# A three-layer graph attention kernel: where a chunk's maxima are started, how its sums are drained, and from where ACT's copies of G come

## The chip, the cores and the metric

One core of a Trainium2 chip. The metric is device time in microseconds of one execution, the median of the runs.

## The reference

Three graph attention layers over N = 3125 nodes, 128 features wide (the hidden width of the first is 256), with 103125 edges and one loop more per node. Cut to what matters:

```python
def gat_layer(x, src, dst, W, a_src, a_dst, b):
    h = x @ W
    e = leaky_relu((h @ a_src)[src] + (h @ a_dst)[dst], 0.2)
    ex = exp(e - segment_max(e, dst)[dst])
    alpha = ex / segment_sum(ex, dst)[dst]
    return segment_sum(alpha[:, None] * h[src], dst) + b

h = relu(layernorm(x))
x = x + gat_layer(relu(gat_layer(h, ..., W1)), ..., W2)     # layers 0 and 1
h = relu(layernorm(x))
x = x + gat_layer(h, ..., W3)                               # layer 2
```

## The kernel before, in words

**Counts.** The first part turns the edge list into a dense matrix C of counts (how often node i points at node j), kept in SBUF as bytes, 125 partitions by 25 tiles by 5 chunks of 625 destinations. The change leaves it alone; it ends at some 242 us.

**Layers.** Each of the 3 layers (L) walks over NC = 5 chunks (c) of 625 destinations, and each chunk over T = 25 steps (s), one per tile of 125 sources. A step needs a tile of weights, 125 sources by 625 destinations: max(r_src, G) times the count, where G is a row of one number per destination, the same on all partitions. DVE makes 15 of the 25 tiles in one instruction each (`product`, L903), from G in PSUM, which TensorE has spread over the partitions by five transposes (`fast_rows`, L1335). For the 10 steps in POOL_S, ACT makes the maximum in three instructions (`row_maximum`, L1135, L1138, L1140) from a copy of G in SBUF (`ga`), and POOL multiplies by the count (`blocks`, L479). The copy: TensorE transposes once more (`copied_rows`, L1344, after step COPY_PE = 6), ACT moves the rows to SBUF (`copy_rows`, L1147, after step COPY_ACT = 8). TensorE then multiplies the tile with the sources' features (`products`, L1354): five destination tiles, two records each in the trace, so ten a step, summed in PSUM over the 25 steps. The tiles lie in a ring of 8 buffers (and a ninth for step 24); DVE and ACT wait on `pe_done` before they overwrite one.

**Maxima.** Each chunk also needs a maximum over all sources: 25 `top_step` instructions of DVE (L777, L780) run into two PSUM buffers, TOP0 and TOP1. A step waits for the last one of its own buffer (`same`), `in_odd` says which buffer it has. `join_tops` (L785) joins the two. `fast_chunk` of DVE starts them AHEAD = 4 steps ahead of the products, two of them after the chunk's last product. TensorE transposes the result (`top_transpose`, L1313, after step 1 of the next chunk, for the last chunk after step 23), DVE reduces it and works out `back` in four parts at the steps CHAIN_AT (`maxima`, L793 to L807); ACT makes `kappa` of it (`factors`, L1056, step 9).

**Drain.** ACT copies the sums from PSUM to `raw` (`move_sums`, L1051 and L1052) at step 3 of the next chunk, behind the row maximum of step 2, once all 25 steps are done; TensorE's step 0 waits for it (`drained`). DVE then makes `rz` in three parts at steps 9, 10 and 11 (`sums_inverse`, L818 to L831). In layer 1 DVE adds the sums to x at step 12 (`residual`, L838, five instructions) and takes the statistics of the layer norm at 13 and 14; POOL works out the scale (L458 to L463), ACT normalises (L1089). Layers 0 and 1 also compute the next layer's features between TensorE's steps (`after_sums`: L1371, L1379, L1387, L1400, L1403).

**Order.** Every engine runs its instructions in the order in which the program lists them: in ACT's `fast_chunk` the row maximum of a step stood ahead of what follows the sums. `fast_rows` for the next chunk comes after TensorE's step ROWS_PE = 23, and waits for all of DVE's products of the chunk, since these read the same PSUM rows. SP only stores the result in layer 2.

## Time and profile before

| what | us |
|---|---|
| median of 3 runs (lowest, highest) | 861.53 (860.94, 868.83) |
| the profiled execution's own time | 867.72 |
| its span in the trace | 866.0 |
| mean granted TensorE clock, share of full speed | 0.904 |
| DVE busy / PE busy / ACT busy / POOL busy | 748.6 / 705.4 / 495.7 / 269.8 |

Numbers of rows are microseconds from the start of the span unless marked ns. Busy times are the sums of an engine's instructions; PE and PEld (its weight loads) overlap.

### The profile page before, as it was taken

The page shows a single profiled execution, that of the slowest core. Times are in us where ns is not written, and L with a number is a line of the kernel's source. Part 1 is how long each engine was busy: PE and PEld are TensorE (multiplying, and loading weights), DVE is VectorE, ACT ScalarE, POOL GpSimd, SP SyncE. Part 2 cuts the span into 40 slices and gives each one's busy share as a digit, 9 for nine tenths or more (in the row PEclk, how much of TensorE's full clock was granted, in tenths as well). Part 3 has the DMA queues.
Part 4 walks back from the last instruction along what each step waited for, and adds up shares of the span by engine and source line. Part 5 has one row for each costly group of instructions (what it writes and reads, how often), then busy time and mean ns, then how long its engine had stood idle before and what let it go on. Part 6 is the DMA issues. An engine that isn't in the chain of part 4 may idle for free.

```text
span 866.0 us, 14422 instructions
## 1 busy us (share of the span) xinstructions
PE 705.4 (81%) x5762; PEld 681.2 (79%) x5762; DVE 748.6 (86%) x1010; ACT 495.7 (57%) x790; POOL 269.8 (31%) x214
## 2 busy tenths in 40 slices
PE   5256889988878898989957989797984798988984
PEld 5256888888868898989957979797974798978984
DVE  5599999999789989898729899989892989999993
ACT  0072444444478765686527856757662787585671
POOL 1512000000025434343303434434340245462563
PEclk9996788888789999999958999898987799999997
DMA  3400000000000000000000000000000000000001
GB/s 97 95 1 1 1 1 1 2 1 1 1 1 2 1 2 1 1 2 1 2 3 1 1 1 2 2 1 1 2 0 4 1 2 1 16 17 1 16 1 33
DMA packets 9554, 6.86 MB, mean 8 GB/s; under 512 B 2108, under 2 KB 9145, under 8 KB 9470
## 3 DMA queue, kind: packets, MB, share of 16 engines
q1 hardware_dynamic: 8670, 4.49, 1.9%
q0 software_dynamic: 800, 1.26, 0.6%
q8 instruction: 52, 0.85, 0.4%
q14 instruction: 32, 0.26, 0.1%
HBM read 4.14 MB, written 1.60 MB: 7 GB/s over the span
## 4 chain that ended last, share of the span: by engine, by line
PE 47%; DVE 30%; issue 9%; ACT 6%; POOL 5%; DMA 2%; DVEq 0%; POOLq 0%; ACTq 0%
PE ps L1354 30%; DVE scratch L617 13%; DVE ps L777 7%; PE ps L1256 7%; DVE scratch L903 4%; POOL scratch L479 2%; ACT scratch L1140 2%; PE ps L1400 2%; PE ps L1216 2%; ACT scratch L1135 1%; PE ps L1379 1%; DMA edge_sb<-in_edges 1%; PE ps L1335 1%; PE ps L1344 1%; PE ps L1263 1%
## 5 line engine op out<-in xcount | busy, mean ns | idle before, releaser
L1354 PE MATMUL ps<-hA,scratch 125*125 125x129 f32 x2500 | 303.4, 280 | 36.3 <-POOL scratch L479 20.9
L1354 PEld LDWEIGHTS ps<-hA,scratch 125*125 125x125 f32 x2500 | 291.2, 192 | 45.5 <-POOL scratch L479 25.2
L479 POOL TENSOR_TENSOR scratch<-scratch 125x625 f32<-125x625 f32 x150 | 209.8, 1402 | 302.5 <-ACT scratch L1140 302.5
L777 DVE SCALAR_TENSOR_TENSOR ps<-C,a_unit,ps 125x625 f32<-125x625 uint8 x330 | 276.1, 860 | 0.5
L903 DVE SCALAR_TENSOR_TENSOR scratch<-ps,r_src,C 125x625 f32<-125x625 f32 x225 | 191.6, 858 | 23.3 <-PE ps L1335 23.3
L1354 PE MATMUL ps<-hB,scratch 125*125 125x129 f32 x1250 | 162.2, 291 | 27.5 <-DVE scratch L903 15.7
L1354 PEld LDWEIGHTS ps<-hB,scratch 125*125 125x125 f32 x1250 | 155.1, 203 | 32.9 <-DVE scratch L903 18.8
L1256 PE MATMUL ps<-scratch 128*128 128x125 bf16 x1250 | 148.4, 296 | 23.3 <-DVE scratch L617 17.2
L1256 PEld LDWEIGHTS ps<-scratch 128*128 128x128 bf16 x1250 | 143.0, 121 | 27.6 <-DVE scratch L617 21.2
L1140 ACT ACTIVATE scratch<-scratch,r_src 125x625 f32<-125x625 f32 x150 | 134.8, 899 | 0.0
L1003 ACT ACTIVATE C<-ps 125x1750 uint8<-125x1750 f32 (+3 forms) x50 | 74.3, 1488 | 98.4 <-PE ps L1256 98.4
L1135 ACT ACTIVATE scratch<-gathered,r_inv 125x625 f32<-125x625 f32 x150 | 121.2, 808 | 0.8 <-PE ps L1354 0.8
L1138 ACT ACTIVATE scratch<-C 125x625 f32<-125x625 uint8 x150 | 107.4, 716 | 4.8 <-POOL scratch L479 4.8
L617 DVE TENSOR_TENSOR scratch<-key_lo,hB 128x6656 bf16<-128x6656 bf16 (+3 forms) x26 | 94.6, 3640 | 4.2 <-PE ps L1256 4.1
L617 DVE TENSOR_TENSOR scratch<-key_col,hB 128x6500 bf16<-128x6500 bf16 (+3 forms) x26 | 85.9, 3304 | 0.0
L470 POOL PARTITION_ALL_REDUCE extg<-ext x3 | 2.8, 926 | 189.1 <-DVE ext L637 189.1
L1147 ACT ACTIVATE gathered<-ps 125x625 f32<-125x625 f32 x15 | 10.4, 692 | 56.0 <-PE ps L1344 56.0
L1051 ACT ACTIVATE scratch<-ps 125x387 f32<-125x387 f32 x15 | 7.4, 492 | 48.4 <-PE ps L1354 48.4
L780 DVE TENSOR_SCALAR ps<-C,a_unit 125x625 f32<-125x625 uint8 x30 | 24.8, 862 | 4.3 <-issue 4.2
L793 DVE TENSOR_REDUCE mu<-ps 125x5 f32<-125x625 f32 x15 | 12.0, 803 | 15.7 <-PE ps L1313 15.7
L634 DVE TENSOR_SCALAR a_neg<-ab 125x25 f32<-125x25 f32 x3 | 0.5, 180 | 28.3 <-ACTq L1205 23.8
L1089 ACT ACTIVATE scratch<-xr,nbias,rstd 125x128 f32<-125x128 f32 x25 | 10.2, 483 | 25.7 <-POOL nbias L463 25.7
(146 smaller groups left out, 478.2 us busy)
## 6 DMA issues: line engine op xcount, KB each, us to landing
xr<-in_x SPq DMA_DIRECT2D x1, 1562.5 KB
out<-xr SPq DMA_DIRECT2D x5, 312.5 KB
edge_sb<-in_edges SPq DMA_DIRECT2D x1, 805.7 KB
w<-in_W SPq DMA_DIRECT2D x2, 128.0 KB
gathered<-in_edges,start_i POOLq DMA_INDIRECT x5, 6.3
w<-in_W SPq DMA_DIRECT2D x1, 64.0 KB
av<-in_a_src SPq DMA_DIRECT2D x4, 0.5 KB
av<-in_a_dst SPq DMA_DIRECT2D x4, 0.5 KB
```

Of the source, the lines that this page charges most:

```text
L479: g.tensor_tensor(slot[s], slot[s], wide[n % 2], ALU.mult).then_inc(pool_done[L], 1)
L617: last = v.tensor_tensor(hot[:, g0:g1, :, :], keys.unsqueeze(2).broadcast_to([128, g1 - g0, m, LANES]), iota_t[:, 0:m, :].unsqueeze(1).bro ...
L777: v.scalar_tensor_tensor(dest, counts, a_unit[:, s:s + 1], top, ALU.min, ALU.max).then_inc(top_done[L], 1)
L780: v.tensor_scalar(dest, counts, a_unit[:, s:s + 1], None, ALU.min).then_inc(top_done[L], 1)
L903: v.scalar_tensor_tensor(slot[s].rearrange("p (t n) -> p t n", n=P), tiles(ROWU), r_src[:, s:s + 1], C5[:, c, s, :].rearrange("p (t n) -> ...
L1003: a_.activation(C5[:, c, :, rows].rearrange("p t (w q) -> p t w q", q=WQ), tiles(at_, w1_ - w0).rearrange("p w (t q) -> p t w q", q=WQ), A ...
L1135: a_.activation(A, ga[c % 2][:, :], ACT.Relu, bias=-1.0, scale=r_inv[:, s:s + 1]).then_inc(over_done[L], 1)
L1138: a_.activation(wide[k % 2], C5[:, c, s, :], ACT.Copy)
L1140: a_.activation(A, A, ACT.Identity, bias=r_src[:, s:s + 1], scale=r_src[:, s:s + 1]).then_inc(rowmax_ok[L], 1)
L1216: last = mm(ps[0:P, CNT + g:CNT + g + 1], before[:, k, P * g:P * (g + 1)], ones_b[:, :], start=(k == 0 and g == 0), stop=(k == NS - 1), sk ...
L1256: last = mm(ps[0:128, o:o + WC], hot_lo[i][:, at_g, :, lane], hot_col[i][:, at_g, :, lane], start=(k == 0), stop=(k == KC - 1))
L1354: last = mm(ps[0:P, acc_at(t):acc_at(t) + HW], A[:, P * t:P * (t + 1)], feat, start=opens and t in (0, 3), stop=closes, skip_group_check=True)
```

## The change

- `in_odd` loses its cases: steps 0 to 4 of a chunk's maxima all go to TOP0, from step 5 on odd ones to TOP1. AHEAD is 5: these five run back to back after a chunk's last product (before the first product, in a layer's first chunk); the other twenty are spread over the steps 0 to 22 by `top_at`, the join follows at step 23.
- The products of steps 23 and 24 are issued together, first both steps for destination tiles 0 to 2, then both for 3 and 4 (`last_products`); a semaphore `acc_half` tells ACT when the first three are done. ACT moves the sums at step 0 instead of 3. `fast_rows` comes after step 22, and the last chunk's `top_transpose` after step 24.
- In ACT's `fast_chunk` the move, `factors` and `after_sums` stand ahead of the row maximum of their step. POOL_S is (3, 5, 7, 9, 11, 14, ...) instead of (2, 4, 6, 9, 11, 13, ...).
- In layer 1, chunks 0 to 3, POOL makes the residual (a product and a sum, 125x640 each) behind its tile of step 11; the statistics move to the steps 15 and 16.
- Only chunk 0's copy of G is made by TensorE and ACT. TensorE transposes g_row to 25 lines of 125, ACT copies them out, SP stores them in DRAM and loads each later chunk's 625 numbers back onto all 125 partitions, as soon as the buffer is free. SP reads the mode flag for it, and DVE waits for that reading before it writes the next.

```diff
+    g_d = nc.dram_tensor("g_lines", (3, T * P), fp32).ap()
-        AHEAD = 4
-        SUMS_AT = 3
+        AHEAD = 5
+        SUMS_AT = 0
-        TOPS_PE, LAST_TOPS = 1, 23
+        TOPS_PE, LAST_TOPS = 1, 24
-        COPY_PE, COPY_ACT = 6, 8
-        ROWS_PE = 23
+        ROWS_PE = 22
-        RESIDUAL_AT, STATS = 12, (13, 14)
-        POST_POOL = [((12, 0),), ((15, 3),), ((12, 0), (15, 1), (18, 2))]
+        STATS = (15, 16)
+        POST_POOL = [((12, 0),), ((12, 2), (17, 3)), ((12, 0), (15, 1), (18, 2))]
-        POOL_S = (2, 4, 6, 9, 11, 13, 16, 18, 20, 22)
+        POOL_S = (3, 5, 7, 9, 11, 14, 16, 18, 20, 22)
-        def in_odd(c, k):
-            if c == 0 and k < AHEAD:
-                return False
-            return k % 2 == (AHEAD - 2) % 2 if k < AHEAD else k > AHEAD and k % 2 == (AHEAD + 1) % 2
+        def in_odd(k):
+            return k >= AHEAD and k % 2 == 1
+        def top_at(k):
+            return (k - AHEAD) * (T - 3) // (T - 1 - AHEAD)
...
+            def ga_load(L, c):
+                if c > 1:
+                    sp.wait_ge(over_done[L], pool_no(c - 1, 0))
+                    sp.wait_ge(ga_loaded[L], 16 * (c - 1))
+                sp.dma_start(ga[c % 2], g_d[L, c * CD:(c + 1) * CD].unsqueeze(0).broadcast_to([P, CD])
+                             ).then_inc(ga_loaded[L], 16)
+            for L in range(LAYERS):
+                sp.wait_ge(mode_ready, L + 1)
+                mode = sp.value_load(fast[0:1, 0:1], min_val=0, max_val=1)
+                sp.sem_inc(mode_read, 1)
+                with sp.If(mode):
+                    sp.wait_ge(lines_ready[L], 1)
+                    sp.dma_start(g_d[L, :].rearrange("(t p) -> t p", p=P), g_lines).then_inc(lines_stored[L], 16)
+                    sp.wait_ge(lines_stored[L], 16)
+                    ga_load(L, 1)
+                    for c in range(NC):
+                        if 0 < c < NC - 1:
+                            ga_load(L, c + 1)
+                        if L == LAYERS - 1 and c:
+                            store(c - 1)
...
+            def residual(c):
+                pool.wait_ge(rz_ready, NC + c + 1)
+                g.tensor_tensor(agg, raw[:, :, 0:D], rz[:, :].unsqueeze(2).broadcast_to([P, CT, D]),
+                                ALU.mult).then_inc(raw_used, 1)
+                pool.wait_ge(raw_used, NC + c + 2)
+                xc = xr[:, c * CT:(c + 1) * CT, :]
+                g.tensor_tensor(xc, xc, agg, ALU.add).then_inc(x_ready, 1)
...
             def fast_chunk(L, c):
                 for s in range(T):
                     if s not in POOL_S:
                         product(L, c, s)
-                    if s or c == 0:
-                        next_top(L, c * T + s + AHEAD)
-                    if s == T - 1:
-                        next_top(L, (c + 1) * T + AHEAD)
+                    for k in range(AHEAD, T):
+                        if top_at(k) == s:
+                            top_step(L, c, k)
+                    if s == top_at(T - 1) + 1:
+                        join_tops(L, c)
...
+                if c < NC - 1:
+                    for k in range(AHEAD):
+                        top_step(L, c + 1, k)
...
-            def move_sums(L, c):
+            def move_sums(L, c, halves=True):
                 n = L * NC + c
-                act.wait_ge(pe_done[L], in_layer(c, T))
                 act.wait_ge(raw_used, n + 1)
+                if halves:
+                    act.wait_ge(acc_half[L], c + 1)
+                else:
+                    act.wait_ge(pe_done[L], in_layer(c, T))
                 a_.activation(raw[:, 0:3, :], acc3[0], ACT.Copy).then_inc(raw_half, 1)
+                if halves:
+                    act.wait_ge(pe_done[L], in_layer(c, T))
                 a_.activation(raw[:, 3:CT, :], acc3[1], ACT.Copy).then_inc(raw_ready, 1)
...
+            def copy_rows(L):
+                act.wait_ge(ga_rows[L], 1)
+                a_.activation(g_lines, ps[0:T, work_at(CT):work_at(CT) + P], ACT.Copy).then_inc(lines_ready[L], 1)
+                a_.activation(ga[0].rearrange("p (t n) -> p t n", n=P), tiles(WORK), ACT.Copy).then_inc(ga_ready[L], 1)
...
-                    if s in POOL_S:
-                        row_maximum(L, c, s)
                     if c:
                         if s == SUMS_AT:
                             move_sums(L, c - 1)
                         if s == KAPPA_AT:
                             factors(L, c - 1)
                         after_sums(L, c - 1, s)
-                    if NP and s == COPY_ACT and c < NC - 1:
-                        copy_rows(L, c + 1)
+                    if s in POOL_S:
+                        row_maximum(L, c, s)
...
+            def last_products(L, c):
+                for t0, t1, out_sem in ((0, 3, acc_half[L]), (3, CT, pe_done[L])):
+                    for s in (T - 2, T - 1):
+                        for t in range(t0, t1):
+                            last = mm(ps[0:P, acc_at(t):acc_at(t) + HW], slot[s][:, P * t:P * (t + 1)],
+                                      h_of[L][:, s, :], start=False, stop=s == T - 1, skip_group_check=True)
...
-                    if NP and s == COPY_PE and c < NC - 1:
-                        copied_rows(L, c + 1)
```

## Rows read from the trace of the kernel before

**Rows 1.** The page: busy time, share of the span and instructions of each engine

```profile
PE 705.4 (81%) x5762; PEld 681.2 (79%) x5762; DVE 748.6 (86%) x1010; ACT 495.7 (57%) x790; POOL 269.8 (31%) x214
```

**Rows 2.** The waits: us in total, times, longest us

```profile
ACT gathered L1147 <- PE ps L1344: 56.0, 15, 4.7
...
PE ps L1354 <- POOL scratch L479: 32.5, 22, 2.6
...
DVE scratch L903 <- PE ps L1335: 23.3, 9, 3.8
...
DVE zk L818 <- ACT kappa L1056: 9.1, 12, 1.0
```

**Rows 3.** SP's waits, in the same columns

```profile
SPq L60 <- DMA out<-xr: 4.7, 1, 4.7
```

**Rows 4.** Timeline: the drains that bound three chunks of layers 0, 1 and 2

```profile
281.35 0.49 ACT L1051 ACTIVATE scratch<-ps 125x387 f32<-125x387 f32 x1 [3.45 <-PE ps L1354]
...
397.26 0.49 ACT L1051 ACTIVATE scratch<-ps 125x387 f32<-125x387 f32 x1 [0.85 <-PE ps L1354]
...
493.55 0.49 ACT L1051 ACTIVATE scratch<-ps 125x387 f32<-125x387 f32 x1 [3.45 <-PE ps L1354]
...
614.99 0.49 ACT L1051 ACTIVATE scratch<-ps 125x387 f32<-125x387 f32 x1 [0.85 <-PE ps L1354]
...
713.64 0.49 ACT L1051 ACTIVATE scratch<-ps 125x387 f32<-125x387 f32 x1 [3.45 <-PE ps L1354]
...
820.38 0.49 ACT L1051 ACTIVATE scratch<-ps 125x387 f32<-125x387 f32 x1 [6.16 <-PE ps L1354]
```

**Rows 5.** Stretches: us, PE, PEld, DVE, ACT, POOL busy (records), PEclk, DMA share, GB/s

```profile
280.30:318.50 38.20, 35.15 (x313) 34.40 (x312) 34.63 (x48) 25.95 (x43) 13.69 (x10) 1.00 0.00 1
...
572.90:614.00 41.10, 35.13 (x283) 34.09 (x282) 37.47 (x64) 26.42 (x45) 15.80 (x14) 0.92 0.01 1
```

**Rows 6.** Timeline around the boundary of layer 1's chunk 3: DVE and PE

```profile
572.94 1.64 DVE L903 SCALAR_TENSOR_TENSOR scratch<-ps,r_src,C 125x625 f32<-125x625 f32 x2 [2.64 <-PE ps L1335]
...
574.61 2.44 PE L1354 MATMUL ps<-hB,scratch 125*125 125x129 f32 x20 [0.68 <-DVE scratch L903]
```

**Rows 7.** Timeline of the same chunk: the copy of G and what follows it

```profile
583.67 0.69 ACT L1147 ACTIVATE gathered<-ps 125x625 f32<-125x625 f32 x1 [4.71 <-PE ps L1344]
...
586.56 1.50 POOL L479 TENSOR_TENSOR scratch<-scratch 125x625 f32<-125x625 f32 x1 [6.00 <-ACT scratch L1140]
586.68 1.40 DVE L818 TENSOR_TENSOR zk<-scratch,kappa 125x5 f32<-125x5 f32 x1 [0.95 <-ACT kappa L1056]
...
588.12 5.77 PE L1354 MATMUL ps<-hB,scratch 125*125 125x129 f32 x50 [2.28 <-POOL scratch L479]
```

**Rows 8.** A stretch of the same chunk, columns as in rows 5

```profile
600.00:604.00 4.00, 3.80 (x18) 3.50 (x18) 4.00 (x6) 4.00 (x9) 2.23 (x3) 0.50 0.00 0
```

**Rows 9.** Timeline of DVE in the last chunks of layers 0 and 1

```profile
396.22 1.64 DVE L903 SCALAR_TENSOR_TENSOR scratch<-ps,r_src,C 125x625 f32<-125x625 f32 x2 [2.54 <-PE ps L1335]
...
424.16 2.41 DVE L903 SCALAR_TENSOR_TENSOR scratch<-ps,r_src,C 125x625 f32<-125x625 f32 x3
...
613.96 1.64 DVE L903 SCALAR_TENSOR_TENSOR scratch<-ps,r_src,C 125x625 f32<-125x625 f32 x2 [2.57 <-PE ps L1335]
...
632.97 1.39 DVE L838 SCALAR_TENSOR_TENSOR xr<-scratch,rz,xr 125x128 f32<-125x128 f32 x5
...
645.73 2.41 DVE L903 SCALAR_TENSOR_TENSOR scratch<-ps,r_src,C 125x625 f32<-125x625 f32 x3
```

**Rows 10.** Timeline: three maxima of one buffer in a row

```profile
242.82 2.69 DVE L777 SCALAR_TENSOR_TENSOR ps<-C,a_unit,ps 125x625 f32<-125x625 uint8 x3
```

**Rows 11.** The groups by line: POOL's sum in layer 2

```profile
L498 POOL TENSOR_TENSOR xr<-xr,scratch 125x640 f32<-125x640 f32 x5 | 6.6, 1319 | 0.1
```

**Rows 12.** Timeline of the end of layer 0

```profile
432.85 1.27 PE L1354 MATMUL ps<-hA,scratch 125*125 125x129 f32 x10
433.05 0.81 DVE L793 TENSOR_REDUCE mu<-ps 125x5 f32<-125x625 f32 x1 [6.47 <-PE ps L1313]
...
435.12 0.17 DVE L818 TENSOR_TENSOR zk<-scratch,kappa 125x5 f32<-125x5 f32 x1 [0.54 <-ACT kappa L1056]
```

More of the change, by code:

```diff
@@ L273, in gat_stack_kernel @@
         kappa_ready = sem("kappa_ready")
+        x_ready = sem("x_ready")
         raw_half = sem("raw_half")
+        acc_half = [sem(f"acc_half{L}") for L in range(3)]
         raw_ready = sem("raw_ready")
@@ L310, in gat_stack_kernel @@
         ga_ready = [sem(f"ga_ready{L}") for L in range(3)]
+        ga_loaded = [sem(f"ga_loaded{L}") for L in range(3)]
+        lines_ready = [sem(f"lines_ready{L}") for L in range(3)]
+        lines_stored = [sem(f"lines_stored{L}") for L in range(3)]
+        mode_read = sem("mode_read")
         h1_sb = sem("h1_sb")
@@ L351, in in_layer @@
             return c * T + s
[L354 removed]
+        POOL_S = (3, 5, 7, 9, 11, 14, 16, 18, 20, 22)
         NP = len(POOL_S)
[L357 to L362 removed]
+        def in_odd(k):
+            return k >= AHEAD and k % 2 == 1
+        LAST_ODD = max(k for k in range(T) if in_odd(k))
+        def top_at(k):
+            return (k - AHEAD) * (T - 3) // (T - 1 - AHEAD)
         def pool_before(s):
@@ L416, in store @@
                 sp.dma_start(out_v[:, bass.ds(c * CT, CT), :], xr[:, bass.ds(c * CT, CT), :]).then_inc(out_done, 16)
-            for L in range(LAYERS - 1):
-                with sp.Fori(0, NC) as c:
-                    rest_loads(L, c)
-            for c in range(NC):
-                rest_loads(LAYERS - 1, c)
-                if c:
-                    store(c - 1)
+            def ga_load(L, c):
[18 more added lines that the diff above has]
+                            store(c - 1)
+                with sp.Else():
+                    for c in range(NC):
+                        rest_loads(L, c)
+                        if L == LAYERS - 1 and c:
+                            store(c - 1)
             store(NC - 1)
@@ L508, in post @@
                     result(c, part)
+                elif part == 2:
+                    residual(c)
                 else:
@@ L544, in _ @@
                     for _at, part in POST_POOL[L]:
-                        post(L, NC - 1, part)
+                        if (L, part) != (1, 2):
+                            post(L, NC - 1, part)
         @block.vector
@@ L762, in top_step @@
                 n = c * (T + 1)
-                odd = in_odd(c, s)
+                odd = in_odd(s)
                 at_ = TOP1 if odd else TOP0
                 top = ps[0:P, at_:at_ + CD]
-                same = [k for k in range(s) if in_odd(c, k) == odd]
+                same = [k for k in range(s) if in_odd(k) == odd]
                 if same:
@@ L857, in after_sums @@
                 if L == 1:
-                    if s == RESIDUAL_AT:
-                        residual(c)
                     if s == STATS[0]:
@@ L1130, in row_maximum @@
                 n, A = in_layer(c, s), slot[s]
-                act.wait_ge(ga_ready[L], c + 1)
                 k = pool_no(c, s)
+                if c:
+                    act.wait_ge(ga_loaded[L], 16 * c)
+                else:
+                    act.wait_ge(ga_ready[L], 1)
                 if c or s >= RING:
-                    act.wait_ge(pe_done[L], n - RING if s < RING else n - (RING - 1) if s < T - 1 else n - (T - 1))
-                a_.activation(A, ga[c % 2][:, :], ACT.Relu, bias=-1.0, scale=r_inv[:, s:s + 1]).then_inc(over_done[L], 1)
+                    act.wait_ge(pe_done[L], n - RING if s < RING else n - (RING - 1))
+                a_.activation(A, ga[c % 2], ACT.Relu, bias=-1.0, scale=r_inv[:, s:s + 1]).then_inc(over_done[L], 1)
                 if k > 1:
@@ L1182, in _ @@
                     if NP:
[L1183 removed]
+                        copy_rows(L)
                     for c in range(NC):
@@ L1356, in products @@
                 last.then_inc(out_sem, 1)
+            def last_products(L, c):
[4 more added lines that the diff above has]
+                                      h_of[L][:, s, :], start=False, stop=s == T - 1, skip_group_check=True)
+                        if t1 == CT:
+                            last.then_inc(out_sem, 1)
+                    if t1 < CT:
+                        last.then_inc(out_sem, 1)
             def rest_steps(L, c):
@@ L1363, in rest_steps, with feat_transposes @@
                                  rest_pe, False, False)
-            def feat_transposes(L, c, source, ready, n, maxima_of, rows_of=0):
+            def feat_transposes(L, c, source, ready, n, maxima_of):
                 pe.wait_ge(ready, n)
                 pe.wait_ge(top_max[L], maxima_of + 1)
-                if NP and rows_of:
-                    pe.wait_ge(ga_ready[L], rows_of)
                 for t in range(CT):
@@ L1445, in fast_chunk @@
                         pe.wait_ge(h_scaled[L], s + 1)
-                    products(slot[s], h_of[L][:, s, :], pe_done[L], s == 0, s == T - 1,
-                             L * NC + c if c and s == 0 else 0)
+                    if s < T - 2:
+                        products(slot[s], h_of[L][:, s, :], pe_done[L], s == 0, False,
+                                 L * NC + c if c and s == 0 else 0)
+                    elif s == T - 1:
+                        last_products(L, c)
                     if c:
```

54 lines of the change are left out of this document (23 added, 31 removed).

## The prediction, made before the changed kernel ran

> **What bounds the kernel now.** I read the page first: DVE is busy 86% of the span, PE 81%, the others far less [rows 1]. With two engines that close, the shares don't say what a stage is worth, so I went on to the waits. The reader should find four there that the change touches [rows 2]: DVE waits 23.3 us in 9 places for the spread rows of G; ACT waits 56.0 us for the transposes of its own copy of G; PE waits 32.5 us for POOL's tiles; DVE waits 9.1 us for kappa. Then the drains as milestones: three chunks take 397.26 - 281.35 = 115.9 us in layer 0, 614.99 - 493.55 = 121.4 in layer 1 and 820.38 - 713.64 = 106.7 in layer 2 [rows 4], so 38.6, 40.5 and 35.6 a chunk. Last the timeline of one chunk of layer 1. At its boundary DVE, which has no other work in its program, sits 2.64 us until the rows come, and PE then sits 0.68 for the drain and the first product [rows 6]. Half way, ACT waits 4.71 us in order to copy G; its next row maximum is late, POOL idles 6.00 us, PE 2.28 us and DVE 0.95 us [rows 7]. Later the same chunk has a stretch at a granted clock of 0.50, that is at 1.2 GHz, with 18 records in 4 us, where 50 took 5.77 us before it [rows 7, 8]. So in layers 0 and 1 neither engine is the bound alone: each has 34 to 37 us of work in 38 to 41, and they wait for each other in turn. Layer 2 is close to what DVE alone needs.
>
> **The change part by part.**
>
> *DVE's floor.* The last chunks show DVE without a boundary in them. Layer 0: from 396.22 to 424.16 + 2.41 = 426.57, 30.35 us; layer 1: from 613.96 to 648.14, 34.18 us [rows 9]. Each holds 21 maxima; the new chunk has 20 before its last product and 5 behind it. One DVE instruction of this size takes 0.78 us behind another (two take 1.64, one about 0.86) [rows 6]; but the five all go to one buffer and each waits for the one before, as three did in 2.69, so 0.90 each, 4.5 us [rows 10]. Layer 0: 30.35 - 0.78 + 4.5 = 34.1. Layer 1 loses the residual too, 1.39: 34.18 - 1.39 - 0.78 + 4.5 = 36.5. Layer 2 has no residual and no statistics; I take layer 0's figure and add for the one instruction more in its inverse and for blocked ones (below): 34.9. Were the five as quick as others, each chunk would be 0.6 shorter.
>
> *The rows at the boundary.* After its last product DVE now has 4.5 us of maxima, not two (1.6 us). PE's five transposes are issued one step of ten records (1.1 us) earlier. The wait of 2.64 was what was left after 1.6 us of cover; 4.5 - 1.6 + 1.1 = 4.0 more covers it, and the longest, 3.8, too. What is late next is PE itself where it has no slack.
>
> *PE's floor in layer 0.* A chunk has 313 records in 35.15 us [rows 5], 0.112 each. The copy's five go: 34.6. The early drain takes the 0.68: DVE's first product is ready when PE has done its 20 last records (2.2 us), and ACT's move of the first half (0.49, [rows 4]) fits under the second half's 8 records. The 2.28 us behind the copy goes, but the row maximum of step 9 now stands behind kappa, which waits for DVE's `back` of step 7: kappa 0.2, row maximum 2.1, POOL 1.5, 3.8 us behind `back`, where PE wants the tile after some 2.7; I put 1.1 us for it (bounds 0 and the old 2.28). Sum 34.6 + 1.1 = 35.7, and 0.1 for hand-overs: 35.8 a chunk, above DVE's 34.1. So layer 0 gains 115.9 - 3 x 35.8 = 8.5 us.
>
> *Layer 1.* PE has 283 records [rows 5], about 31.5 us at full clock, and then waits for POOL: the residual puts 2 x 1.32 us [rows 11] ahead of the tile of step 14, and the norm's scale ahead of step 18, each later for PE by up to 1.5 us. PE has 5 us of slack for that, so DVE's 36.5 stands, if the clock holds. With a stretch at 1.2 GHz in it I reckon 38. Bounds 36.5 and 38.5; I take 37.2, nearer to the first: 121.4 - 111.6 = 9.8 us.
>
> *Layer 2.* 106.7 - 3 x 34.9 = 2.0 us.
>
> *The first chunks.* Three boundaries lose a wait of 2.6 on average (23.3 / 9) [rows 2]. ACT loses the copy and the wait for it. Ahead of the first product stand a fifth maximum (0.9, on the path) and a small transpose and copy of G's lines (between 0.2 and 0.7; ACT has time for it). 2.0 each, 6.0 us. Bounds 3 and 9.
>
> *The last chunks.* PE ended layer 0 at 434.12, and zk came at 435.12 [rows 12], 1.0 later, since the maxima had been transposed one step earlier. Now the five transposes follow the last product (0.7), then the chain from L793 to zk, 2.07 us: 2.8 less 0.2 for the earlier move. PE's end is 0.6 earlier, as the transposes left its way: 1.0 us lost a layer, 3.0 in all. In return the last chunk of layer 1 loses a residual on DVE and a good part of its slow stretch, 3.4 us, that of layer 2 gains 1.3, that of layer 0 nothing. Net +1.7 us (bounds -3 and +5).
>
> *The transfer.* SP has nothing else to do until layer 2's stores. The only transfer of this size whose landing shows is the last store: SP waits 4.7 us for it [rows 3]. The load is asked for when the chunk's predecessor's row maxima are done, a whole chunk (35 us) before it is needed; even five times the store's 4.7 us, 24 us, would hide. Cost 0 (bounds 0 and 1 for SP's reading of the flag, which DVE waits for only one layer later). Without the cover, each would cost its landing. POOL's other idle time hides the residual.
>
> **A rule against moving the residual.** DVE's zk, five numbers a partition, took 1.40 us while POOL's tile ran from 586.56 to 588.06, and 0.17 when POOL was idle [rows 7, 12]. So an instruction of DVE can lose a whole POOL instruction. The Trainium skill, SBUF — State Buffer, section "Who interferes with whom", has it as a rule: a DVE instruction with two SBUF inputs and a GpSimd instruction that reads SBUF exclude each other for the whole instruction. This trace agrees. By that rule the residual saves DVE nothing if its time comes back as such waits, which is the second rival below.
>
> **The sum.** 8.5 + 9.8 + 2.0 + 6.0 + 1.7 = 28.0 us. The profiled execution took 867.72 us (span 866.0 and 1.7 around it), so it would take 839.7. The median of the runs is 861.53, 6.2 below; the same gain gives 833.5 us, 3.3% less. A measurement of this kernel can tell about 1% from no change.
>
> **The rivals.**
>
> *PE becomes the bound at a falling clock (0.25).* In layers where DVE leads, PE now waits at the boundary for the last product, does 25 records, and waits again for the first product behind five maxima: 4.5 + 0.86 - 0.7 - 2.2, about 2.4 us idle, each chunk. Such a wait (2.28), followed by another, came before the stretch at 0.50 [rows 7, 8]. Against it: a PE that lags has no such gap. If it costs 1.7 us in each chunk of layer 0, 1.8 in layer 1 and 1 in layer 2 over my figures, 3 x 4.5 = 13.5 us come back: 847. [...]
>
> *DVE is blocked by a denser POOL (0.12).* So far POOL is idle when DVE's small instructions of steps 5 to 7 run; without the copy's stall it isn't. One blocked instruction more in each of the 12 later chunks at 1.2 us: 14 us back, 848. Against it: the last chunks, which have no copy, held one or two such waits and are in my floors.
>
> *The wait only moves (0.07).* The rows now come before PE's last two steps, so the next step 0 is later by 1.1 us, and if that and step 9's wait are not hidden under DVE, layers 0 and 1 keep their pace: only the first chunks' 6 and layer 2's 2, less the tail's 3, about 5 us: 856.
>
> *Slower (0.06).* The same gap at the boundary, but with PE at 1.2 GHz for so long that the ring of 8 is full and DVE stops. Each record costs 0.11 us more; 45 slow records are 5 us. In layer 1 PE has 31.5 us of work at full clock and some 3 us of waits; from 55 slow records on (of 283), 34.5 + 6 passes the old 40.5. With 75 a chunk in all layers I get 34.5 + 8.3 = 42.8 in layer 1, 43 in layer 0 and 38 in layer 2: 3 x (4.4 + 2.3 + 2.4) = 27 worse, less 5: 883. I see no such run of slow records now, hence the low chance.
>
> **How the numbers follow.** My forecast has 0.50, its own range 827 to 841. Faster by over 1%: the forecast, the first two rivals (0.87), less a little for their far ends: 0.86. Within 1%: 0.08. Slower: 0.06. The lower end of the range takes layer 1 at 36.5 (2), step 9 without a gap in layer 0 (3), the first chunks' and tail's better bounds (4): about 824. The upper end takes in the falling clock and the blocked DVE: 851.
>
> **What would show it.** Right: DVE's wait for the rows all but gone (under 4 us in place of 23.3); no wait of ACT for transposes of a copy but one a layer; drains 35 to 36 us apart in layer 0, about 37 in layer 1, 35 in layer 2; five maxima at 0.9 in a row; the mean clock at or over 0.90; the gap from PE's last product to zk 2.6 us. Wrong: PE's waits for POOL at step 9 still above 2 us; zk, rz or m_top at 1.4 us oftener than once a chunk; ACT's first row maximum of a chunk waiting for SP's load; more stretches at 0.50 right behind the boundaries.

## The result, and the profile after

| | before | after |
|---|---|---|
| median (lowest to highest), us | 861.24 (858.94 to 868.83), 4 runs | 833.63 (833.27 to 834.56), 4 runs |
| profiled execution; its span, us | 867.72; 866.0 | 833.74; 831.8 |
| mean granted clock | 0.904 | 0.923 |

The ratio is 0.9658, 95% interval 0.9615 to 0.9702: faster, and the median lies 0.1 us from the forecast. The profiled executions gained 34.0 us, though, where my sum had 28.0. Both can't be right for the reasons that I gave, and most of what follows is about that.

The page of the changed kernel: busy times, and the clock in 40 slices.

```profile
PE 680.1 (82%) x5705; PEld 658.9 (79%) x5705; DVE 739.7 (89%) x990; ACT 490.1 (59%) x781; POOL 270.2 (32%) x222
...
PEclk9996887889779999999998999999996799999997
...
gathered<-g_lines SPq DMA_DIRECT2D x12, 305.2 KB
```

PE has 57 records less, DVE 20 instructions less (the residual, five in each of four chunks) [rows 1]. Its waits (us in total, times, longest):

```profile
PE ps L1396 <- POOL scratch L506: 28.3, 22, 1.5
...
DVE scratch L945 <- PE ps L1379: 5.1, 6, 1.4
...
ACT gathered L1193 <- PE ps L1386: 3.8, 2, 2.1
...
DVE zk L858 <- ACT kappa L1101: 1.0, 3, 0.3
```

Against [rows 2], DVE's wait for the rows fell from 23.3 to 5.1, ACT's for the copy from 56.0 to 3.8 and DVE's for kappa from 9.1 to 1.0. Under 4 us was what I had named for the rows; it is 5.1. PE's wait for POOL hardly moved: 32.5 to 28.3. No compute engine waits for SP's twelve loads; SP itself waits for them to land, 26.7 us in all and 4.1 us at the longest.

One middle chunk of layer 0 and one of layer 1 (columns as in [rows 5]):

```profile
313.70:349.90 36.20, 34.69 (x308) 34.06 (x308) 34.59 (x48) 25.75 (x43) 14.57 (x11) 1.00 0.03 10
551.80:588.10 36.30, 31.89 (x277) 30.75 (x277) 35.86 (x58) 25.91 (x43) 17.68 (x16) 1.00 0.00 1
```

In layer 0 PE is busy 34.69 of 36.2 us, with 308 records; in layer 1 DVE is busy 35.86 of 36.3. The clock is full in both, where layer 1 before had 0.92. The timeline of the first of them, PE, DVE, ACT and POOL, tells what is left:

```profile
309.58 3.60 DVE L817 SCALAR_TENSOR_TENSOR ps<-C,a_unit,ps 125x625 f32<-125x625 uint8 x4
...
314.28 2.37 PE L1405 MATMUL ps<-hA,scratch 125*125 125x129 f32 x20
314.55 0.87 DVE L945 SCALAR_TENSOR_TENSOR scratch<-ps,r_src,C 125x625 f32<-125x625 f32 x1 [1.37 <-PE ps L1379]
315.86 0.49 ACT L1094 ACTIVATE scratch<-ps 125x387 f32<-125x387 f32 x1 [2.13 <-PE ps L1405]
...
325.16 0.21 ACT L1101 ACTIVATE kappa<-back 125x5 f32<-125x5 f32 x1 [1.74 <-DVE back L847]
...
327.37 0.16 DVE L858 TENSOR_TENSOR zk<-scratch,kappa 125x5 f32<-125x5 f32 x1
...
327.57 1.51 POOL L506 TENSOR_TENSOR scratch<-scratch 125x625 f32<-125x625 f32 x1 [2.78 <-ACT scratch L1188]
...
329.13 4.67 PE L1396 MATMUL ps<-hA,scratch 125*125 125x129 f32 x40 [1.49 <-POOL scratch L506]
329.69 1.29 POOL L506 TENSOR_TENSOR scratch<-scratch 125x625 f32<-125x625 f32 x1 [0.61 <-ACT scratch L1188]
329.84 1.16 DVE L871 TENSOR_TENSOR rz<-zk,kappa 125x5 f32<-125x5 f32 x1
```

Three things are to be seen. The dependent maxima run at 0.90 us (four in 3.60), yet DVE still waits 1.37 us for the rows. PE's only gap, 1.49 us, comes from ACT, which waits for `back` ahead of kappa and has step 9's row maximum behind it. And zk, which took 1.40 us before in nine of fifteen chunks, takes 0.16; but rz, five numbers a partition as well, now takes 1.16 beside the POOL tile that began at 329.69.

To find where the time went I use DVE's zk as a mark, and PE's first rows of a layer:

```profile
291.23 0.16 DVE L858 TENSOR_TENSOR zk<-scratch,kappa 125x5 f32<-125x5 f32 x1
...
399.65 0.16 DVE L858 TENSOR_TENSOR zk<-scratch,kappa 125x5 f32<-125x5 f32 x1
...
426.98 0.17 DVE L858 TENSOR_TENSOR zk<-scratch,kappa 125x5 f32<-125x5 f32 x1 [0.34 <-ACT kappa L1101]
...
442.59 0.80 PE L1379 MATMUL ps<-ident,g_row 125*125 125x125 f32 x5 [3.98 <-ACT e_src L1063]
...
491.75 0.16 DVE L858 TENSOR_TENSOR zk<-scratch,kappa 125x5 f32<-125x5 f32 x1
...
600.95 0.16 DVE L858 TENSOR_TENSOR zk<-scratch,kappa 125x5 f32<-125x5 f32 x1
...
628.50 0.17 DVE L858 TENSOR_TENSOR zk<-scratch,kappa 125x5 f32<-125x5 f32 x1 [0.34 <-ACT kappa L1101]
```

| gain in us, layers 0 / 1 / 2 | predicted | first profile of before | third profile of before (below) |
|---|---|---|---|
| first rows to first zk | 2.0 / 2.0 / 2.0 | 2.7 / 3.7 / 3.8 | 2.9 / 3.8 / 3.8 |
| three middle chunks | 8.5 / 9.8 / 2.0 | 7.4 / 12.2 / 3.5 | 7.5 / 8.6 / 3.6 |
| last chunk to its zk | -1.0 / 2.4 / 0.3 | -2.1 / 1.6 / -1.0 | -2.1 / -0.3 / -1.0 |
| between the layers, both gaps | 0 | 2.7 | 1.8 |
| sum | 28.0 | 34.5 | 28.5 |

### The profile page after: what moved, and what is told of

Read it like the earlier page. It is cut to its first block, busy times and chain, and to the rows that moved or that the text cites. A ratio compares the mean times of both kernels' runs of the same rounds, so it can differ in the third digit from the quotient of the medians.

```text
span 831.8 us, 14225 instructions
## 1 busy us (share of the span) xinstructions
PE 680.1 (82%) x5705; PEld 658.9 (79%) x5705; DVE 739.7 (89%) x990; ACT 490.1 (59%) x781; POOL 270.2 (32%) x222
## 4 chain that ended last, share of the span: by engine, by line
DVE 43%; PE 32%; issue 12%; ACT 7%; POOL 4%; DMA 2%; DVEq 0%; POOLq 0%; ACTq 0%
DVE ps L817 16%; PE ps L1396 14%; DVE scratch L655 13%; PE ps L1300 7%; DVE scratch L945 7%; PE ps L1405 2%; ACT scratch L1188 2%; DVE ps L820 2%; PE ps L1260 2%; POOL scratch L506 2%; PE ps L1452 1%; PE ps L1431 1%; ACT scratch L1183 1%; DMA edge_sb<-in_edges 1%; ACT scratch L1134 1%
## 5 line engine op out<-in xcount | busy, mean ns | idle before, releaser
L1396 PE MATMUL ps<-hA,scratch 125*125 125x129 f32 x2300 | 273.9, 279 | 29.2 <-DVE scratch L945 17.1
L506 POOL TENSOR_TENSOR scratch<-scratch 125x625 f32<-125x625 f32 x150 | 200.1, 1337 | 292.4 <-ACT scratch L1188 283.6
L1396 PEld LDWEIGHTS ps<-hA,scratch 125*125 125x125 f32 x2300 | 265.1, 192 | 35.7 <-DVE scratch L945 20.2
L817 DVE SCALAR_TENSOR_TENSOR ps<-C,a_unit,ps 125x625 f32<-125x625 uint8 x330 | 279.1, 863 | 1.9
L945 DVE SCALAR_TENSOR_TENSOR scratch<-ps,r_src,C 125x625 f32<-125x625 f32 x225 | 193.6, 860 | 5.1 <-PE ps L1379 5.1
L1300 PE MATMUL ps<-scratch 128*128 128x125 bf16 x1250 | 148.4, 296 | 23.3 <-DVE scratch L655 17.1
L1300 PEld LDWEIGHTS ps<-scratch 128*128 128x128 bf16 x1250 | 143.0, 121 | 27.6 <-DVE scratch L655 21.1
L1396 PE MATMUL ps<-hB,scratch 125*125 125x129 f32 x1150 | 139.4, 279 | 22.4 <-POOL scratch L506 16.3
L1396 PEld LDWEIGHTS ps<-hB,scratch 125*125 125x125 f32 x1150 | 132.8, 191 | 27.8 <-POOL scratch L506 20.6
L1101 ACT ACTIVATE kappa<-back 125x5 f32<-125x5 f32 x15 | 3.1, 207 | 42.7 <-DVE back L847 42.7
L1405 PE MATMUL ps<-hA,scratch 125*125 125x129 f32 x200 | 23.7, 273 | 0.2 <-DVE scratch L945 0.2
```

What stands on the lines that cost most here:

```text
L506: g.tensor_tensor(A, A, wide[n % 2], ALU.mult).then_inc(pool_done[L], 1)
L817: v.scalar_tensor_tensor(dest, counts, a_unit[:, s:s + 1], top, ALU.min, ALU.max).then_inc(top_done[L], 1)
L945: v.scalar_tensor_tensor(slot[s].rearrange("p (t n) -> p t n", n=P), tiles(ROWU), r_src[:, s:s + 1], C5[:, c, s, :].rearrange("p (t n) -> ...
L1300: last = mm(ps[0:128, o:o + WC], hot_lo[i][:, at_g, :, lane], hot_col[i][:, at_g, :, lane], start=(k == 0), stop=(k == KC - 1))
L1396: last = mm(ps[0:P, acc_at(t):acc_at(t) + HW], A[:, P * t:P * (t + 1)], feat, start=opens and t in (0, 3), stop=closes, skip_group_check=True)
L1405: last = mm(ps[0:P, acc_at(t):acc_at(t) + HW], slot[s][:, P * t:P * (t + 1)], h_of[L][:, s, :], start=False, stop=s == T - 1, skip_group_c ...
```

## The experiments

Twelve runs: nine edited kernels, the changed kernel once more and the kernel before twice more. The kernel before was timed beside each group. "The changed kernel" is the one predicted (833.6 us; 834.4 in its second series). A chunk's period is read from one zk to the next.

**1. The transfer undone.** PE and ACT copy G for every chunk, as before, after steps 6 and 8; the rest stays changed. Cut to what matters:

```diff
-                            ga_load(L, c + 1)
...
+                    if s == 8 and c < NC - 1:
+                        copy_rows(L, c + 1)
...
+                    if s == 6 and c < NC - 1:
+                        copied_rows(L, c + 1)
```

> The changed kernel with ACT's copies of G made as before (five transposes after step 6, ACT's copy at step 8, no transfer). My theory: PE does 5 records more a chunk (0.6 us), and ACT's copy stands ahead of kappa and the row maximum of step 9, so PE's wait for POOL there grows from 1.49 to about 3 us. Layers 0 and 1, where PE's end sets the boundary, lose about 2 us a chunk, layer 2 nothing, the first chunks 1.5 each: 849 us, 15 over the 833.6 (bounds 843 to 854). Rival, the boundary is all and the copy's stall was hidden anyway: at most 837.

848.15 us (844.69 to 849.31); ratio to before 0.9772 (0.9714 to 0.9830). Its waits:

```profile
ACT gathered L1186 <- PE ps L1382: 41.2, 15, 4.8
PE ps L1392 <- POOL scratch L500: 39.3, 21, 2.6
...
DVE scratch L939 <- PE ps L1374: 18.4, 9, 4.9
```

The size is as I expected, the places are not. Layer 0 lost 3.0 us in its first middle chunk and 1.4 in the others (37.6 against 36.14), the first chunks 2.3 to 2.7 each, and 3.2 us were lost between layers 0 and 1 (taken up below). But layer 1's middle chunks took 36.2 (two of them 36.13) and layer 2's 34.22, slightly less than with the transfer (36.40 and 34.67): beside the later POOL tile rz took 0.69 us in layer 1, not 1.16, and 0.51 in layer 2, not 0.96. In the middle chunks where DVE leads, the copy cost nothing.

**2. The residual back on DVE**, five instructions at step 12; POOL's part, (12, 2), goes.

```diff
-        POST_POOL = [((12, 0),), ((12, 2), (17, 3)), ((12, 0), (15, 1), (18, 2))]
+        POST_POOL = [((12, 0),), ((17, 3),), ((12, 0), (15, 1), (18, 2))]
...
+                    if s == 12:
+                        residual(c)
```

> The changed kernel with layer 1's residual back on DVE at step 12 (the statistics stay at 15 and 16). My theory: layer 1 is bound by DVE, 1.39 us more in each of 4 chunks, a little less where PE was the last: 838 us, 4.5 over the 833.6 (bounds 836.5 to 840). Rival, the rule of the shared port: what DVE saved comes back as blocked instructions and a late POOL, so no difference, 833 to 834.5.

844.35 us (843.41 to 847.86), ratio 0.9755 (0.9698 to 0.9812): more than my upper bound. DVE and POOL at that step:

```profile
534.46 1.29 POOL L506 TENSOR_TENSOR scratch<-scratch 125x625 f32<-125x625 f32 x1 [0.83 <-ACT scratch L1186]
535.12 2.89 DVE L878 SCALAR_TENSOR_TENSOR xr<-scratch,rz,xr 125x128 f32<-125x128 f32 x5
536.58 1.29 POOL L506 TENSOR_TENSOR scratch<-scratch 125x625 f32<-125x625 f32 x1 [0.83 <-ACT scratch L1186]
```

The five took 1.39 us in the last chunk of the kernel before [rows 9] and 1.58 to 1.59 in its middle chunks, and 2.89 here for each of the chunks 0 to 3, where they lie across two tiles; for chunk 4's own sums, behind the layer's last product with POOL idle, they took 1.40. A chunk of layer 1 took 39.18 us, 2.8 more. So the blocking that I held against the move speaks for it: in this denser kernel the residual on DVE costs twice its own time. The Trainium skill, SBUF — State Buffer, section "Who interferes with whom", has it that a DVE instruction with two inputs in SBUF and a GpSimd (POOL) instruction that reads SBUF contend for ports that they share, and that these are an exclusive lock. These rows agree: the first of the five took 0.78 us and the fifth 1.41, against 0.34 for each of the three between.

**3. The early drain undone**: the last two steps in the old order, one wait ahead of ACT's two copies.

```diff
-            def move_sums(L, c, halves=True):
+            def move_sums(L, c, halves=False):
...
-                for t0, t1, out_sem in ((0, 3, acc_half[L]), (3, CT, pe_done[L])):
-                    for s in (T - 2, T - 1):
...
+                for s in (T - 2, T - 1):
+                    products(slot[s], h_of[L][:, s, :], pe_done[L], False, s == T - 1)
```

> The changed kernel without the early drain: steps 23 and 24 one after the other, the move of the sums waits for both. My theory: ACT's move (0.49 us and its hand-overs) shows again as about 0.7 us of PE's time a chunk, on the path in layer 0 and mostly in layer 1, hidden in layer 2: 838 us (bounds 836 to 840). Rival, the drain lies beside DVE's product: 833.6, within 1.

838.69 us (837.03 to 840.30), ratio 0.9671 (0.9615 to 0.9726). The total fits, but only 0.4 us a chunk were lost in layer 0 (36.53) and 0.5 in layer 1 (36.88), nothing in layer 2 (34.67); 2.9 us of its 6.2 us longer span lie between layers 0 and 1. I had put 0.68 on it. Not all of the rest is PE's wait for the drain, either: with the chunk's start shifted, DVE's e_top and m_top lay beside tiles of POOL and took 0.37 us longer between them, 0.65 in one chunk of layer 1, and that chunk lost 0.66 where the other two lost 0.38 and 0.39. In layer 1, where DVE leads, this accounts for the whole loss; in layer 0 the two parts are not told apart.

**4. The rows two steps later.**

```diff
-        ROWS_PE = 22
+        ROWS_PE = 24
```

> The changed kernel with the spread rows of G issued behind the products of steps 23 and 24 (ROWS_PE 24) instead of behind step 22; the five maxima at the boundary stay. My theory: the rows come 2.2 us later; layer 1 has 0.3 of DVE's wait now and gets 2.1 to 2.5, layer 0 has PE wait 0.9 for the first product, layer 2 covers all: 4 x 2 + 4 x 0.9 = 11 us, 845 us (bounds 840 to 848). Rival, the five maxima are the whole cover and the place of the rows is nothing: at most 836.

849.21 us (847.70 to 850.92), ratio 0.9797 (0.9741 to 0.9852), above my upper bound. DVE at a boundary of layer 1:

```profile
526.32 0.87 DVE L945 SCALAR_TENSOR_TENSOR scratch<-ps,r_src,C 125x625 f32<-125x625 f32 x1 [2.62 <-PE ps L1379]
```

Two steps are 20 records, 2.2 us, and each boundary of layers 0 and 1 lost just that: chunks of 38.35 and 38.57 us, waits of 3.57 and 2.5 us. There was no spare cover in either layer. In layer 2 (34.67) there was.

**5. Three maxima at the boundary, not five.**

```diff
-        AHEAD = 5
+        AHEAD = 3
```

> Three maxima of the next chunk behind the last product, not five; the two others go back among the products, where they are not dependent on one another. The rows still come one step early. My account: the cover was the sum of both, 4.0 us over what the old wait needed, and the changed kernel's own trace shows 1.37 us of wait left in layer 0 and 0.3 in layer 1. Two maxima less are 1.8 us less cover, but DVE's last product is then about 1.6 us later against the same rows, so the wait hardly changes: 833.6 plus or minus 1.5 us, the wait for the rows at 1.4 to 2.0 us in layer 0. Rival, the five maxima are themselves what hides the rows: each of 12 boundaries loses up to 1.8 us, 845 to 855 us, and DVE's waits for the rows come back to over 15 us in all.

841.48 us (839.90 to 843.77), ratio 0.9731 (0.9668 to 0.9793). My account failed. The time lies between it and the rival's, and the rival had DVE's waits for the rows right: 15.6 us in all. DVE behind its last product in layer 1:

```profile
515.68 1.78 DVE L817 SCALAR_TENSOR_TENSOR ps<-C,a_unit,ps 125x625 f32<-125x625 uint8 x2
519.70 0.87 DVE L945 SCALAR_TENSOR_TENSOR scratch<-ps,r_src,C 125x625 f32<-125x625 f32 x1 [2.23 <-PE ps L1379]
```

With five maxima DVE worked 5 x 0.90 and waited 0.30 us, 4.8 in all; with three it worked 3 x 0.90 and waits 2.1 to 2.2, 4.8 to 4.9 again. In layer 1 the rows come 4.8 us behind DVE's last product either way, so each maximum that is taken from there opens the wait by its own time, and comes back among the products: 37.8 us a chunk, 1.4 more. In layer 0 the rows' place moved (5.8 us behind the last product with five, 5.0, 6.6 and 5.0 with three), the waits were 2.4, 4.0 and 2.4 us, and the chunks took 36.8, 38.4 and 36.8. In layer 2 the chunk even gained 0.3 (34.4), and the first chunks 1.0 each. Another 3.2 us of loss lie between layers 0 and 1 (18.8 us against 15.6).

**6. Row maximum ahead of kappa at step 9.**

```diff
-                        if s == KAPPA_AT:
-                            factors(L, c - 1)
                         after_sums(L, c - 1, s)
                     if s in POOL_S:
                         row_maximum(L, c, s)
+                    if c and s == KAPPA_AT:
+                        factors(L, c - 1)
```

> ACT takes step 9's row maximum first and kappa behind it, in place of the other way round. In the changed kernel PE waits 1.49 us at step 9 of every later chunk for POOL's tile. My account (PE is the bound in layer 0, and that gap is 1.1 of its 35.8 us): the gap goes, and layer 0 gains about 1.2 us in each of 4 chunks, layer 1 and 2 under 0.3 a chunk, since DVE leads there: 828 us (826 to 830). zk may be blocked by POOL's tile again or wait for kappa, which costs DVE up to 1.2 us a chunk. Rival (the gap is slack that PE gives back elsewhere, DVE is the bound in layer 0 too): within 1 us of 833.6.

824.55 us (824.42 to 825.15), ratio 0.9533 (0.9475 to 0.9592): 9.1 us better than the changed kernel, and below the range that I had given. Its stretches (a chunk of layer 0, one of layer 1), then its rz:

```profile
312.91:347.45 34.54, 34.52 (x307) 34.00 (x306) 33.59 (x49) 25.60 (x43) 14.58 (x11) 1.00 0.03 10
544.43:579.78 35.35, 32.09 (x277) 30.86 (x276) 34.86 (x59) 25.79 (x43) 17.70 (x16) 1.00 0.00 1
```

```profile
329.01 0.16 DVE L871 TENSOR_TENSOR rz<-zk,kappa 125x5 f32<-125x5 f32 x1
```

In layer 0 PE is now busy 34.52 of 34.54 us: the gap was on the path, all of it. Layer 1 gained 1.0 us a chunk, which I had not expected: POOL's tile ends before rz, so rz takes 0.16 us in place of 1.17, and DVE leads there. In layer 2 rz fell from 0.96 to 0.16 too, but a chunk gained only 0.2, for another of DVE's small instructions met a tile of POOL in its place:

```profile
L836 DVE SCALAR_TENSOR_TENSOR e_top<-mu,span,b_low 125x5 f32<-125x5 f32 x1 | 0.8, 833 | 0.0
```

It had taken 225 ns there in the changed kernel (the group of that line, one chunk of layer 2).

**7. The last maxima transposed behind step 23 again.**

```diff
-        TOPS_PE, LAST_TOPS = 1, 24
+        TOPS_PE, LAST_TOPS = 1, 23
```

> Only the last chunk of each layer: PE transposes the joined maxima behind step 23 again, ahead of the last products, not behind them. My account put 1.0 us a layer on this: zk 1.0 us earlier behind PE's last product in each layer, 830.6 us (829.5 to 832). Rival (the transposes only delay PE's last products and these set the end): no gain, 833.6.

828.74 us (828.20 to 830.55), ratio 0.9587 (0.9527 to 0.9646). zk came 1.1, 1.1 and 1.8 us earlier in the last chunks; 1.8 us more came from between layers 0 and 1. PE's end and zk in layer 0:

```profile
423.16 2.37 PE L1405 MATMUL ps<-hA,scratch 125*125 125x129 f32 x20
...
426.14 0.17 DVE L858 TENSOR_TENSOR zk<-scratch,kappa 125x5 f32<-125x5 f32 x1 [1.26 <-ACT kappa L1101]
```

Here zk comes 0.6 us behind PE's last product; in the changed kernel it was 426.98 - 424.53 = 2.45.

**8. The five maxima alternating between the two buffers.**

```diff
-        def in_odd(k):
-            return k >= AHEAD and k % 2 == 1
...
+        def in_odd(c, k):
+            if k < AHEAD:
+                return bool(c) and k in (0, 2)
+            return k % 2 == 1
```

> The five maxima behind the last product alternate between the two PSUM buffers again, so that none waits for the one right before it. They take 0.90 us each in the changed kernel and should take 0.79: 0.5 us less at each boundary. My account: DVE leads in layers 1 and 2, so 8 boundaries gain 0.4 to 0.5 us; in layer 0 the rows are late anyway and the wait grows by what the maxima lose: 830 us (829 to 832). Rival (the rows bound all three layers): within 1 us of 833.6, and the wait for the rows grows by 0.5 at every boundary.

837.03 us (834.13 to 838.67), ratio 0.9671 (0.9607 to 0.9734). The rival's mechanism held in layers 0 and 1: the chunks kept their pace (36.16 and 36.42), and the wait for the rows grew by 0.4 us at each boundary, to 1.77 in layer 0 and 0.72 to 0.82 in layer 1. Its time did not: the median is 3.4 us above the changed kernel's, not within 1. Of the profiled span's 3.2 us more, 2.0 lie between layers 0 and 1; in layer 2, which has no such wait, a chunk took 34.79, 0.1 more, and e_top 0.73 us in place of 0.22.

**9. Edits 6 and 7 together, and the changed kernel again beside it.**

> Both edits that gained alone: ACT's row maximum of step 9 ahead of kappa (9.1 us by the medians) and the last chunk's maxima transposed behind step 23 (4.9 us, of which 1.8 was the clock behind layer 0). They touch different chunks, so they should add: 36.16 - 1.6 a chunk in layer 0, 36.36 - 1.0 in layer 1, and zk 1.1 us (layers 0 and 1) and 1.8 us (layer 2) earlier in the last chunks. 824.6 - 4.0 = 820.6 us, between 818.5 and 822.5 by what the clock does behind layer 0. Rival (the last chunk's gain comes from the same wait of PE): 823 to 825.

> The changed kernel unaltered, beside the kernel before on the same chip as the best version. If the 833.6 us belong to the kernel and not to one chip: 832 to 836 us, and a ratio to before between 0.960 and 0.970. From the last zk of layer 0 to layer 1's first rows it had 15.6 us, and the variants 13.8 to 18.8: if this is a matter of the single execution, its runs spread by 2 to 3 us; if of the program, the profile shows 15.6 again.

820.71 us (817.36 to 824.00), ratio 0.9479 (0.9438 to 0.9521), against 834.38 (833.63 to 836.24), ratio 0.9630 (0.9590 to 0.9670), for the changed kernel on the same chip. The two edits add up: this version beats both kernels. The rerun has a second profile, of 836.24 us, and differs from the first in one place. The stretch from layer 0's last zk to layer 1's first rows, in the changed kernel's first profile:

```profile
426.98:442.59 15.61, 7.56 (x45) 6.76 (x46) 3.78 (x21) 4.23 (x13) 0.37 (x1) 0.89 0.02 4
```

in its second:

```profile
426.57:445.06 18.49, 10.68 (x46) 9.41 (x46) 3.78 (x21) 4.23 (x13) 0.38 (x1) 0.55 0.01 3
```

and with edit 7:

```profile
426.14:439.96 13.82, 6.00 (x45) 5.21 (x46) 3.78 (x21) 4.22 (x13) 0.37 (x1) 1.00 0.02 5
```

DVE, ACT and POOL do the same in the same time; PE's 45 records take 6.00, 7.56 or 10.68 us at a mean granted clock of 1.00, 0.89 or 0.55. Between the two profiles of the changed kernel the 2.9 us belong to the single execution, since the program is the same. For the 13.8 us this isn't shown: both kernels with edit 7 have it (13.82 and 13.81), and none of the others, which lie at 15.2 to 18.8, so edit 7 may have a part in it. I count no difference in this stretch for or against an edit.

**10. The kernel before, twice more.** On every chip its runs lay between 859 and 870 us, most of them near one of the two ends.

> The kernel before, unaltered, for a second profile. Its runs so far lie at 859 to 862 and at 864 to 869 us, and the profile that the prediction was made from (867.7) is one of the upper ones. If a stage sets this, it should be the stretch between the layers, where the granted clock fell to 0.50: near 860 us that stretch would be 2 to 3 us shorter and a layer's chunks unchanged; near 867 everything as in the first profile. Rival: the chunks themselves differ, by 0.4 us each.

868.44 us. The stretch between the layers took 17.5 us, less than in the first profile (18.3), and the three middle chunks of layer 1 took 40.9 each. So that stretch was not the cause.

> The kernel before once more. Its second profile (868.44) had 17.5 us between layer 0 and layer 1, 18.3 in the first, and chunks of 40.9 us in layer 1: the stretch between the layers did not make it long. What is left of the 8 us between its two levels should be in layer 1, where a part of each chunk ran at a granted clock of 0.50: if this execution is near 860 us, its chunks of layer 1 should be about 39 us, those of layers 0 and 2 unchanged at 38.6 and 35.6. If it is near 868 again, layer 1 shows 40.5 to 41 us a chunk, and the lower level stays open.

862.81 us, and here is the stage that differs. Two chunks of layer 1 in this third profile:

```profile
532.25:571.49 39.24, 33.76 (x283) 32.83 (x282) 37.45 (x63) 26.28 (x45) 15.85 (x14) 0.96 0.01 1
571.49:610.73 39.24, 33.66 (x283) 32.56 (x282) 37.45 (x64) 26.30 (x45) 15.82 (x14) 0.96 0.01 1
```

and the same two in the first profile, the one predicted from:

```profile
531.82:572.94 41.12, 35.15 (x283) 34.11 (x282) 37.44 (x64) 26.36 (x45) 15.82 (x14) 0.92 0.00 1
572.94:614.00 41.06, 35.09 (x283) 34.05 (x282) 37.47 (x64) 26.38 (x45) 15.80 (x14) 0.92 0.01 1
```

The same 283 records and the same DVE work, but PE had a longer piece at 1.2 GHz. A chunk of this layer has two rhythms, 39.2 and 41 us. The first profile's first such chunk took 39.3, the others 41; the second profile had only the slow rhythm, the third only the fast one. The layer's last chunk goes with them: from its first product to its zk it took 42.8 us in the first two profiles and 41.0 in the third. The time between the rhythms shows as DVE's wait for the rows at the boundaries behind the three middle chunks: 0.76 to 0.88 us after the fast ones, 2.39 to 2.64 after the slow ones. Three or four chunks at 1.8 us are 5 to 7 of the 8 us between the two levels; the stretch between the layers can give the rest. Why an execution falls into one rhythm or the other stays open. The changed kernel's middle chunks of layer 1 ran at 1.00 in both its profiles, its runs within 1.3 us in one series and 2.6 in the other.

## Why the prediction was right, and what in it was wrong

**The median.** It was right to 0.1 us, and part of that is two errors that cancel. I made the sum against an execution of the upper level, and it came out 6 us too small there; then I moved it down by 6.2 us, the distance to the median, as if the changed kernel had to lie as far below its own profile. Most of that distance (some 5.5 us) was three chunks of layer 1 in the slow rhythm, which the changed kernel does not show: it has its profile (833.74) at its median (833.63). So the gain over the profiled execution was 34.0, not 28.0, and over an execution of the lower level it was 862.81 - 833.74 = 29.1. Beside the 11 runs of before in the last series (median 868.61) the same kernel gains 34.2 us, beside the first four 27.6. The direction and some 3 to 4% hold on each; the exact agreement does not.

**PE's floor held.** PE's 34.6 us for layer 0 was measured at 34.69, its rate of 0.112 too. The period of 35.8 was 36.14, since the gap behind kappa was 1.49 and not 1.1; experiment 6 shows that this gap was the whole difference between PE's work and the period. Layer 2's 34.9 was 34.7. DVE's 34.1 for layer 0 is not tested, since PE led; DVE was busy 34.59 us there, and 33.59 in experiment 6, where rz was not blocked.

**Layer 1 was mis-sized.** I put 37.2, between a floor of 36.5 and 38.5 at a slow stretch; it was 36.4, at full clock. The 0.7 above the floor was for a slow stretch that did not come. DVE led the layer, as I said: taking 1.0 us from rz took 1.0 from the chunk. The floor of 36.5 agrees with 36.4, but by errors that cancel. The stretch of the kernel before from which I read it [rows 9] holds two instructions that took over 1 us beside POOL:

```profile
622.58 1.14 DVE L800 SCALAR_TENSOR_TENSOR m_top<-e_top 125x5 f32<-125x5 f32 x1
...
630.12 1.38 DVE L831 TENSOR_TENSOR rz<-zk,kappa 125x5 f32<-125x5 f32 x1
```

In the changed kernel only rz is left, at 1.16, and m_top takes 0.16: the floor had 1.2 us too much. On the other side that stretch holds 20 maxima and the join, not 21 maxima, as many as the new chunk has before its last product, so the 0.78 should not have come off; and I had no wait for the rows, where 0.3 is left. Together 36.5 - 1.2 + 0.8 + 0.3 = 36.4. And the base, 40.5, was mostly the slow rhythm: from 39.2 the gain is 2.8 a chunk, 8.6 in three, close to the 9.8 by which I had it.

**The rows at the boundary: right outcome, wrong reason.** I wrote that 4.0 us more cover a wait of 2.64, and the longest, 3.8, too. The wait went from 23.3 to 5.1, but 1.4 us stayed in layer 0, and experiments 4 and 5 show that nothing was left over in layers 0 and 1: two steps later cost 2.2, a maximum less opened layer 1's wait by 0.9. I had taken the rows' arrival as fixed and DVE's work as filling up to it. In layer 1 PE has waited for POOL's tile of step 20, and from there has the steps 20 to 22 and the new features to do before the transposes:

```profile
546.44 2.47 PE L1396 MATMUL ps<-hB,scratch 125*125 125x129 f32 x20 [1.31 <-POOL scratch L506]
```

DVE's last product ended at 547.05 and the rows came at 551.77, 4.7 us behind it, and in experiment 5 also 4.7 to 4.8, however DVE spends that time; what DVE does there moves the rest of its chunk. A cover has to be counted against the engine that ends the wait, at the pace it then has.

**The drain** I put at 0.68; undone it cost 0.4 in layer 0, 0.5 in layer 1 and 0 in layer 2, and in layer 1 that was DVE's blocked instructions and not the wait.

**The first chunks** were too low: 6.0 us for the three, 10.2 measured, above my upper bound of 9. The copy's part, for which I had given no figure of its own, is 2.3 to 2.7 of 2.7 to 3.8 us each (experiment 1). **The last chunks** were too high, +1.7 against -1.5: the tail's own loss was 1.1, 1.1 and 1.8, as sized (1.0 each) or somewhat more, but the last chunks have the gap at step 9 as well (with edit 6 that of layer 0 took 1.6 us less), which I had left out of them. These two errors nearly cancel.

**The transfer** costs nothing that shows: there is no wait of ACT for it, as forecast. Undoing it costs 14.5 us, of which 3.2 lie between the layers.

**The residual** I priced at 1.39 us, the quickest of the old ones; in the changed kernel it is worth 2.8 a chunk, so the price of this edit depends on the others. The four costs, 14.5, 10.7, 15.6 and 5.1 us, make 46 for a gain of 28 to 34 together, but that alone shows no dependence: the 15.6 are for two row steps where the change made one, and 3.2 and 2.9 us of the others lie between the layers. Half of the one and the rest of the others are some 32.

**The rivals.** A falling clock (0.25) did not come; the mean clock rose from 0.904 to 0.923. Nor did the slower kernel (0.06). A short fall need not cost anything where DVE leads: with the copy back (experiment 1) one chunk of layer 1 ran at a mean of 0.95 and the next at 1.00, both in 36.13 us. A longer one did cost in the kernel before (39.2 us at 0.96, 41.1 at 0.92). Blocked DVE instructions (0.12) did come, once a chunk: rz at 1.16, but in exchange zk was freed (1.40 to 0.16), so the count stayed. Waits that only move: in part, PE's wait for POOL (28.3 of 32.5 us) was the largest thing left, and its part at step 9, with rz's block, was worth 9.1 us.

## What to carry to other kernels

Before summing gains against a profile, find out which of the kernel's levels that execution belongs to, and which stage makes the difference: a change that removes that stage's stall also removes the distance between profile and median. Behind a wait for a small value on one engine, look for the producer of another engine's tile: reordering two instructions of ACT, with nothing removed, was worth a third of the whole change (9.1 us to 27.6). Where DVE and POOL share a stretch, a short DVE instruction can cost as much as POOL's beside it (zk took 0.16 us or 1.40), so move either the work or the time at which POOL starts.

## What the runs showed of the hardware that I had not expected

- The same 45 records of PE, between two layers, took 7.56 us in one execution of the changed kernel and 10.68 in another, and the whole stretch 15.6 and 18.5, at a mean granted clock of 0.89 and 0.55; with edit 7 they took 6.00, and the stretch 13.8, at 1.00.
- A loop can settle into a clock rhythm that repeats: the kernel before ran chunks of 39.2 us at a mean clock of 0.96, or of 41.1 at 0.92, for three or four chunks in a row, with equal work.
- The cost of the blocking depends on how the instructions lie: rz, 125x5, took 0.16, 0.51, 0.69, 0.96 or 1.17 us by when POOL's tile started, and five DVE instructions of 125x128 took 1.39 to 1.40, 1.59 or 2.89. An edit that frees one small instruction can hand the block to another, as rz to e_top in layer 2.
